# The causal mask of the first attention: added by VectorE on the way out of PSUM instead of accumulated by TensorE, with the reciprocal of the sums moved

## The chip, the cores and the metric

The kernel runs on one core of a Trainium2 chip. The metric is the device time of one execution in microseconds, the median of the timed runs; lower is better. A profiled execution records every instruction of every engine, and each of its durations and waits is taken from there.

## The reference, cut to what matters

Four blocks follow each other on an activation of 2048 tokens by 128 features: a windowed attention with global tokens, a memory layer, a second attention with rotary positions, and a mixture of experts. The change touches only the first attention. For the normalised input `x` (2048 x 128), 16 heads of 64 and windows of 128 tokens it is:

```
q, k, v = x @ wq, x @ wk, x @ wv                  # 16 heads of 64
gk, gv  = g_tok @ wk, g_tok @ wv                  # 32 global rows
att  = q_window @ k_window^T * SCALE              # 128 x 128 for each window and head
att  = where(upper triangle, neg, att)            # the causal mask
local_out  = softmax(att) @ v_window
global_out = softmax(q @ gk^T * SCALE) @ gv       # a softmax of its own, not masked
x = x + (local_out + global_out) @ wo
```

## The kernel before, in words

`attn0_block` works on 8 pairs of heads and 16 windows of 128 tokens: 128 steps, one for each pair and window. A round (`ROUND = 32`) is two pairs. Five engines each run their own list of instructions, written out by hand in the same order of steps (`step(r, i)`), and semaphores hold them together. There is no planner: the order in the code is the order on each engine, and an engine that waits holds up everything behind it in its list.

What step `i` does, engine by engine:

- **TensorE** (`pe`): the scores of window `i` for the two heads of the pair (L345: two products of 128 queries with 160 columns, 128 local keys and 32 global ones, each in its own PSUM bank, issued as four instructions since float32 takes two each). Then the mask (L349): four bf16 products of a split identity with a split mask matrix, which add -1e30 above the diagonal into the same banks. Then the transposes of the probabilities of window `i-2` (L363), the product of the probabilities of window `i-3` with the values (L375 and L377, called PV below), the output projection of window `i-4` (L388), and in 12 of 16 steps a piece of the q, k or v projection of the next pair (L326, L329, L322; `job`). The first of these 12 has the projection of the global rows in front (L315, L316). The last pair has no next one, so its 16 steps have no such piece.
- **VectorE** (`dve`): first the piece of k or v that the step before projected (L464, L472). Then it waits for the scores and takes the negated row maxima of the local part (L488, 256 elements in each partition, both heads) and of the global part (L489, 64 elements). In the one step per pair with global rows it saves them (`save_globals`, L456 and L458). Then the reciprocal of the sums of window `i-1` (L497), for which it waits for ScalarE's exponentials of that window; the copy of the transposed probabilities of window `i-2` (L503); and in every fourth step the addition to `x` (L510).
- **ScalarE** (`act`): a piece of q if there is one (L535). Then it waits for the maxima of window `i` and computes four exponentials with their sums: for each head the local one (L548, 128 elements, read from PSUM) and the global one (L550, 32 elements), each followed by the read-out of its sum. After them the copy of the output of window `i-3` out of its single PSUM bank (L558, `oT`).
- **GpSimd** (`pool`): multiplies the probabilities by the reciprocals (L580), both parts, and so releases the transposes.

The waits that matter here: the scores of step `i` overwrite the banks of step `i-2` and wait for its exponentials. PV of step `i` writes the one output bank and so waits until ScalarE has copied the output of PV of the step before, which stands in ScalarE's list behind the exponentials of the step before:

```
    pe.wait_ge(pt_saved, r * ROUND + w + 1)
    if w >= 1:
        pe.wait_ge(o_saved, r * ROUND + w)          # PV of window w, in step w + 3
```

and in ScalarE's list

```
    mm.then_inc(exp_ready, 1)                       # the four exponentials of window i
    w = i - 3
    act.wait_ge(o_ready, r * ROUND + w + 1)
    nc.scalar.activation(oT[:, w % 4, :], m.psum[:, O_B, 0:P], ACT.Copy).then_inc(o_saved, 1)
```

The first q piece of a pair waits until VectorE has saved the global rows (`g_saved`), as it uses the same PSUM bank. `setup_block` fills the constants on GpSimd while SyncE issues the first loads.

Of the kernel before, what the change touches and what calls it, by code (L numbers as in the profile page):

```python
# [7 lines left out]
BF16 = mybir.dt.bfloat16  # L8
# [3 lines left out]
ALU = mybir.AluOpType  # L12
# [138 lines left out]
def setup_block(nc, m, a):  # L151

    with ExitStack() as ctx:
# [25 lines left out]
        def _(pool):  # L179
            nc.gpsimd.memset(m.ident[:, :], 0.0).then_inc(zeroed, 1)  # L180
            nc.gpsimd.memset(m.identb[:, :], 0.0).then_inc(zeroed, 1)
            nc.gpsimd.memset(m.split_ident[:, :, :], 0.0).then_inc(zeroed, 1)
            nc.gpsimd.memset(m.split_mask[:, :, :], 0.0).then_inc(zeroed, 1)
# [3 lines left out]
            pool.wait_ge(zeroed, 7)  # L187
            for c in range(NC):
                nc.gpsimd.memset(m.wo_last[c * VCOLS:c * VCOLS + 1, D:D + 1], 1.0).then_inc(zeroed, 1)
            pool.wait_ge(zeroed, 11)  # L190
# [5 lines left out]
            for part in range(2):  # L196
                for g0 in (0, P // 2):
                    rows = slice(g0, g0 + P // 2)
                    pool.wait_ge(patterned, 2 + 2 * (2 * part + g0 // (P // 2)))
                    i, w = m.split_ident[rows, part, :], m.split_mask[rows, part, :]  # L200
                    nc.gpsimd.affine_select(out=i, in_=i, compare_op=ALU.not_equal, fill=1.0,
                                            base=part * P // 2, pattern=[[-1, P]], channel_multiplier=1).then_inc(patterned, 1)
                    nc.gpsimd.affine_select(out=w, in_=w, compare_op=ALU.is_ge, fill=MASKED,
                                            base=part * P // 2, pattern=[[-1, P]], channel_multiplier=1).then_inc(patterned, 1)


def attn0_block(nc, m, a, loads):
# [3 lines left out]
    with ExitStack() as ctx:  # L211
        def sb(name, shape, dt=F32):
            return ctx.enter_context(nc.sbuf_tensor(name, shape, dt))
# [11 lines left out]
        nmax = sb("nmax", [P, 4, 4])  # L225
        total = sb("total", [P, 4, 4])
# [23 lines left out]
        max_ready, exp_ready = sem("max_ready"), sem("exp_ready")  # L250
# [58 lines left out]
        def _(pe):  # L309
# [22 lines left out]
            def step(r, i, more=True):  # L332
                if i < ROUND or more:
# [10 lines left out]
                    for j in range(2):  # L344
                        nc.tensor.matmul(m.psum[:, bank + j, 0:WL], qs[half[j], b, s * P:(s + 1) * P], kx[half[j], b, s, :],  # L345
                                         start=True, stop=False)
                    for part in range(2):
                        for j in range(2):
                            mm = nc.tensor.matmul(m.psum[:, bank + j, 0:P], m.split_ident[half[j], part, :],  # L349
                                                  m.split_mask[half[j], part, :], start=False, stop=(part == 1))  # L350
# [123 lines left out]

# [1240 lines left out]
```

## Time and profile before

| what | value |
|---|---|
| runs shown, us | 1282.47, 1283.92, 1284.54 (median 1283.92) |
| the profiled execution, its own time | 1284.34 us |
| its span | 1282.6 us |
| TensorE busy in the span | 1224.7 us (95%) |
| first attention, from its first scores to its last step | 28.6 to 360 us |
| granted clock of TensorE from 28.6 to 33, from 33 to 36, from 50 to 340 us | 1.00, 0.54, 1.00 |
| TensorE busy from 28.6 to 33 us | 2.24 of 4.40 us |
| set-up: SyncE's last issue ends, GpSimd's last select ends | 5.95 us, 5.99 us |

The span runs from the first to the last recorded instruction, and the execution's own time is 1.74 us longer. Busy time is what an engine spent in instructions; a share near 100% says that an engine is full, not that it does nothing needless. In the timeline each row has a start, a duration and, in brackets, the idle time ahead of it with the instruction that ended it. The instructions of one line that follow each other are merged into one row with their count; the duration then runs from the first start to the last end. Consecutive instructions of VectorE and ScalarE overlap a little: the next one starts before the recorded end of the last.

### The profile page before, as it was taken

The page shows a single profiled execution, that of the slowest core. Times are in us where ns is not written, and L with a number is a line of the kernel's source. Part 1 is how long each engine was busy: PE and PEld are TensorE (multiplying, and loading weights), DVE is VectorE, ACT ScalarE, POOL GpSimd, SP SyncE. Part 2 cuts the span into 40 slices and gives each one's busy share as a digit, 9 for nine tenths or more (in the row PEclk, how much of TensorE's full clock was granted, in tenths as well). Part 3 has the DMA queues.
Part 4 walks back from the last instruction along what each step waited for, and adds up shares of the span by engine and source line. Part 5 has one row for each costly group of instructions (what it writes and reads, how often), then busy time and mean ns, then how long its engine had stood idle before and what let it go on. Part 6 is the DMA issues. An engine that isn't in the chain of part 4 may idle for free. (4 is left out here: it accounts for less than half of the span.)

```text
span 1282.6 us, 26536 instructions
## 1 busy us (share of the span) xinstructions
PE 1224.7 (95%) x10153; PEld 667.2 (52%) x10153; DVE 975.1 (76%) x1668; ACT 878.0 (68%) x2401; POOL 185.7 (14%) x366
## 2 busy tenths in 40 slices
PE   6999999999986879999999999999999999998999
PEld 5777777777864643433333333333333333334677
DVE  6666666666677869899999999999999999935300
ACT  3566566666746520488888888888888888885542
POOL 2333333333354130000000000010000000000100
PEclk9999999999997985699999999999999999999999
DMA  3100000000000030001110001100011000000100
GB/s 83 74 10 10 7 4 10 10 1 4 2 1 1 1 146 35 27 20 47 38 39 29 24 27 39 38 29 23 27 38 39 30 24 25 22 6 1 37 17 17
DMA packets 24891, 34.04 MB, mean 27 GB/s; under 512 B 6685, under 2 KB 18749, under 8 KB 22526
## 3 DMA queue, kind: packets, MB, share of 16 engines
q1 hardware_dynamic: 24766, 32.35, 7.6%
q8 instruction: 81, 1.33, 0.5%
q14 instruction: 44, 0.36, 0.1%
HBM read 24.86 MB, written 5.24 MB: 23 GB/s over the span
## 5 line engine op out<-in xcount | busy, mean ns | idle before, releaser
L1231 DVE TENSOR_REDUCE rowmax<-psum 128x1 f32<-128x1024 f32 x512 | 618.0, 1224 | 29.8 <-PE psum L1094 22.3
L1336 ACT ACTIVATE pb<-psum 128x512 f32<-128x512 f32 x1024 | 555.7, 596 | 78.9 <-PE psum L1136 58.3
L1094 PE MATMUL psum<-kf,qf 64*128 64x512 f32 x1024 | 393.0, 467 | 5.0 <-DVE rowmax L1231 3.9
L1136 PE MATMUL psum<-qf,kf 64*128 64x512 f32 x1024 | 377.1, 448 | 0.8 <-DMA qf<-nT 0.8
L1121 PE MATMUL psum<-pb,vx 128*32 128x256 f32 x4096 | 327.4, 392 | 3.6 <-issue 3.6
L1136 PEld LDWEIGHTS psum<-qf,kf 64*128 64x128 f32 x1024 | 153.7, 186 | 209.4 <-ACT pb L1336 190.8
L1121 PEld LDWEIGHTS psum<-pb,vx 128*32 128x32 f32 x4096 | 81.4, 108 | 188.5 <-ACT pb L1336 96.8
L1094 PEld LDWEIGHTS psum<-kf,qf 64*128 64x128 f32 x1024 | 161.3, 195 | 29.7 <-DVE rowmax L1231 24.4
L548 ACT ACTIVATE pr<-psum,nmax 128x128 f32<-128x128 f32 x256 | 93.8, 366 | 114.4 <-DVE nmax L489 114.3
L580 POOL TENSOR_TENSOR pr<-pr,rtotal 128x256 f32<-128x256 f32 (+1 forms) x256 | 110.5, 452 | 235.9 <-DVE rtotal L497 235.9
L488 DVE TENSOR_REDUCE nmax<-psum 128x2 f32<-128x256 f32 x128 | 53.8, 420 | 65.0 <-PE psum L349 65.0
L1370 POOL CAST nparts<-nfull 128x16 fp32r<-128x16 f32 x16 | 3.1, 196 | 623.7 <-DVE nfull L1240 623.7
L377 PE MATMUL psum<-pt,vz 128*128 128x128 f32 x512 | 78.5, 276 | 0.0
L550 ACT ACTIVATE pr<-psum,nmax 128x32 f32<-128x32 f32 x256 | 73.0, 285 | 0.0
L345 PE MATMUL psum<-kx,qs 64*128 64x160 f32 x512 | 69.8, 350 | 1.7 <-ACT pr L550 1.7
L363 PE MATMUL psum<-ident,pr 128*128 128x128 f32 x384 | 70.4, 292 | 0.7 <-POOL pr L580 0.7
L503 DVE COPY pt<-psum 128x384 f32<-128x384 f32 x128 | 67.9, 531 | 1.8 <-PE psum L363 1.6
L377 PEld LDWEIGHTS psum<-pt,vz 128*128 128x128 f32 x512 | 67.9, 193 | 0.0
L345 PEld LDWEIGHTS psum<-kx,qs 64*128 64x128 f32 x512 | 38.8, 185 | 52.9 <-ACT pr L550 39.2
L1523 ACT ACTIVATE hT<-psum,b 128x512 f32<-128x512 f32 x48 | 32.4, 688 | 40.6 <-PE psum L1538 40.5
L550 ACT ACTIVATION_READ_ACCUMULATOR pr<-psum,nmax 128x1 f32 x256 | 53.0, 207 | 0.0
L375 PE MATMUL psum<-pt,gv 128*128 128x128 f32 x256 | 51.4, 283 | 0.3 <-ACT oT L558 0.2
(220 smaller groups left out, 1370.7 us busy)
## 6 DMA issues: line engine op xcount, KB each, us to landing
qf<-q_parts SPq DMA_DIRECT2D x62, 128.0 KB
kf<-k_parts SPq DMA_DIRECT2D x62, 128.0 KB
k_parts<-parts SPq DMA_DIRECT2D x4, 512.0 KB, 3.3
q_parts<-parts SPq DMA_DIRECT2D x4, 512.0 KB, 3.9
x<-in_L_attn_x SPq DMA_DIRECT2D x2, 512.0 KB, 4.7
cos<-cos_table SPq DMA_DIRECT2D x1, 1024.0 KB
sin<-sin_table SPq DMA_DIRECT2D x1, 1024.0 KB
sumsT<-acc SPq DMA_DIRECT2D x60, 16.0 KB
```

The costliest lines, as they stand in the source:

```text
L345: nc.tensor.matmul(m.psum[:, bank + j, 0:WL], qs[half[j], b, s * P:(s + 1) * P], kx[half[j], b, s, :], start=True, stop=False)
L363: mm = nc.tensor.transpose(m.psum[:, T_B, j * P:(j + 1) * P], pr[:, w % 4, j * P:(j + 1) * P], m.ident[:, :])
L377: mm = nc.tensor.matmul(ob, vz[:, b, j, s, :], pt[:, w % 2, j * P:(j + 1) * P], start=False, stop=(j == 1))
L503: nc.vector.tensor_copy(pt[:, w % 2, :], m.psum[:, T_B, 0:TW]).then_inc(pt_saved, 1)
L548: nc.scalar.activation(pr[:, i % 4, j * P:(j + 1) * P], sc[:, 0:P], ACT.Exp, bias=nmax[:, i % 4, j:j + 1], accum_out=total[:, i % 4, j:j + 1])
L550: mm = nc.scalar.activation(pr[:, i % 4, 2 * P + j * G0:2 * P + (j + 1) * G0], sc[:, P:WL], ACT.Exp, bias=nmax[:, i % 4, 2 + j:3 + j], acc ...
L580: mm = nc.gpsimd.tensor_tensor(prw, prw, rb, ALU.mult)
L1094: mm = nc.tensor.matmul(m.psum[:, M_B + (u % 2) * 2 + n % 2, :], qf[ROWS, b, t * P:(t + 1) * P], kf[ROWS, b, c * BANK:(c + 1) * BANK], sta ...
L1121: mm = nc.tensor.matmul(m.psum[c * VCOLS:(c + 1) * VCOLS, A_B, cols], vx[:, h % VB, t, :], pb[:, (h * NT + t) % 3, c, cols], start=(t == 0 ...
L1136: nc.tensor.matmul(m.psum[:, bank, :], kf[SCORES, b, t * P:(t + 1) * P], qf[SCORES, b, c * BANK:(c + 1) * BANK], start=True, stop=True).th ...
L1231: nc.vector.tensor_reduce(rowmax[:, g % 2, u // 2, u % 2:u % 2 + 1], m.psum[:, M_B + (u % 2) * 2:M_B + (u % 2) * 2 + 2, :].rearrange("p b ...
L1336: nc.scalar.activation(pb[:, s % 3, c, :], m.psum[:, bank_of[(s, c)], :], ACT.Exp, scale=SCALE).then_inc(exp_ready, 1)
```

## The change

The mask is no longer multiplied in by TensorE. A float32 mask of 128 x 128 (0 and -1e30) is built once. In each step VectorE adds it to the local scores of both heads as it reads them from PSUM and writes the masked scores to a new SBUF tile, `masked` (four windows deep). Behind this addition stands the reciprocal for window `i-1`, which stood behind the maxima (and behind `save_globals`). Then come the maximum of the global part from PSUM and the maximum of the local part, now from `masked`, for which VectorE waits on a semaphore of its own addition. The order of the two maxima is swapped. ScalarE's local exponentials read `masked` in SBUF instead of PSUM; its global ones are as before. The rest of the block is as it was.

```diff
@@ setup_block, gpsimd
-            nc.gpsimd.memset(m.split_ident[:, :, :], 0.0).then_inc(zeroed, 1)
-            nc.gpsimd.memset(m.split_mask[:, :, :], 0.0).then_inc(zeroed, 1)
+            nc.gpsimd.memset(m.mask[:, :], 0.0).then_inc(zeroed, 1)
...
-            for part in range(2):
-                for g0 in (0, P // 2):
...
-                    nc.gpsimd.affine_select(out=i, in_=i, compare_op=ALU.not_equal, fill=1.0, ...
-                    nc.gpsimd.affine_select(out=w, in_=w, compare_op=ALU.is_ge, fill=MASKED, ...
+            pool.wait_ge(patterned, 2)
+            nc.gpsimd.affine_select(out=m.mask[:, :], in_=m.mask[:, :], compare_op=ALU.is_ge, fill=MASKED,
+                                    base=0, pattern=[[-1, P]], channel_multiplier=1).then_inc(patterned, 1)
@@ attn0_block, tensor, step
                     for j in range(2):
-                        nc.tensor.matmul(m.psum[:, bank + j, 0:WL], qs[half[j], b, s * P:(s + 1) * P], kx[half[j], b, s, :],
-                                         start=True, stop=False)
-                    for part in range(2):
-                        for j in range(2):
-                            mm = nc.tensor.matmul(m.psum[:, bank + j, 0:P], m.split_ident[half[j], part, :],
-                                                  m.split_mask[half[j], part, :], start=False, stop=(part == 1))
+                        mm = nc.tensor.matmul(m.psum[:, bank + j, 0:WL], qs[half[j], b, s * P:(s + 1) * P], kx[half[j], b, s, :],
+                                              start=True, stop=True)
                     mm.then_inc(scores_ready, 1)
@@ attn0_block, vector, step
+            def invert_sums(r, i, more):
+                w = i - 1
+                if 0 <= w < ROUND or (w >= ROUND and more):
+                    dve.wait_ge(exp_ready, r * ROUND + w + 1)
+                    nc.vector.reciprocal(rtotal[:, w % 4, :], total[:, w % 4, :]).then_inc(rtotal_ready, 1)
...
-                    nc.vector.tensor_reduce(nmax[:, i % 4, 0:2], smw[:, :, 0:P], AX_X, ALU.max, negate=True)
-                    nc.vector.tensor_reduce(nmax[:, i % 4, 2:4], smw[:, :, P:WL], AX_X, ALU.max,
+                    nc.vector.tensor_tensor(masked[:, i % 4, :, :], smw[:, :, 0:P],
+                                            m.mask[:, :].rearrange("p (o k) -> p o k", o=1).broadcast_to([P, 2, P]),
+                                            ALU.add).then_inc(masked_ready, 1)
+                invert_sums(r, i, more)
+                if i < ROUND or more:
+                    nc.vector.tensor_reduce(nmax[:, i % 4, 2:4], smw[:, :, P:WL], AX_X, ALU.max, negate=True)
+                    dve.wait_ge(masked_ready, r * ROUND + i + 1)
+                    nc.vector.tensor_reduce(nmax[:, i % 4, 0:2], masked[:, i % 4, :, :], AX_X, ALU.max,
                                             negate=True).then_inc(max_ready, 1)
                 if job(i, more) and job(i, more)[1:] == (0, "q"):
                     save_globals(r, job(i, more)[0], J_B)
-                w = i - 1
-                if 0 <= w < ROUND or (w >= ROUND and more):
-
-                    dve.wait_ge(exp_ready, r * ROUND + w + 1)
-                    nc.vector.reciprocal(rtotal[:, w % 4, :], total[:, w % 4, :]).then_inc(rtotal_ready, 1)
@@ attn0_block, scalar, step
-                        nc.scalar.activation(pr[:, i % 4, j * P:(j + 1) * P], sc[:, 0:P], ACT.Exp,
+                        nc.scalar.activation(pr[:, i % 4, j * P:(j + 1) * P], masked[:, i % 4, j, :], ACT.Exp,
                                              bias=nmax[:, i % 4, j:j + 1], accum_out=total[:, i % 4, j:j + 1])
```

## Rows read from the trace of the kernel before

**Rows 1.** Busy time by stretch; columns as in the first line.
```profile
core 0: us, PE busy (x) PEld busy (x) DVE busy (x) ACT busy (x) POOL busy (x), PEclk, DMA share, GB/s
50.00:340.00 290.00, 290.00 (x2429) 224.94 (x2428) 177.54 (x564) 181.34 (x1014) 94.62 (x220) 1.00 0.02 6
...
375.00:380.00 5.00, 4.16 (x17) 1.37 (x18) 4.16 (x18) 3.00 (x5) 4.08 (x3) 1.00 0.02 5
```

**Rows 2.** Timeline of a step without a projection: start, duration, engine, line.
```profile
202.03 0.30 PEld L375 LDWEIGHTS psum<-pt,gv 128*128 128x128 f32 x2
...
203.12 0.54 PE L345 MATMUL psum<-kx,qs 64*128 64x160 f32 x4
...
203.49 0.28 PE L349 MATMUL psum<-split_mask,split_ident 64*128 64x128 bf16 x4
...
203.70 0.55 PE L363 MATMUL psum<-ident,pr 128*128 128x128 f32 x3
203.81 0.42 DVE L488 TENSOR_REDUCE nmax<-psum 128x2 f32<-128x256 f32 x1 [1.03 <-PE psum L349]
...
204.15 0.21 DVE L489 TENSOR_REDUCE nmax<-psum 128x2 f32<-128x64 f32 x1
...
204.28 0.17 DVE L497 RECIPROCAL rtotal<-total 128x4 f32<-128x4 f32 x1
...
204.40 0.37 ACT L548 ACTIVATE pr<-psum,nmax 128x128 f32<-128x128 f32 x1 [0.61 <-DVE nmax L489]
...
205.07 0.54 PE L345 MATMUL psum<-kx,qs 64*128 64x160 f32 x4
...
205.53 0.21 ACT L550 ACTIVATION_READ_ACCUMULATOR pr<-psum,nmax 128x1 f32 x1
205.62 0.29 ACT L558 ACTIVATE oT<-psum 128x128 f32<-128x128 f32 x1
...
206.02 0.30 PEld L375 LDWEIGHTS psum<-pt,gv 128*128 128x128 f32 x2
```

**Rows 3.** Timeline: scores and local maxima behind a k piece, then a v piece.
```profile
213.47 0.54 PE L345 MATMUL psum<-kx,qs 64*128 64x160 f32 x4
...
214.19 0.41 DVE L488 TENSOR_REDUCE nmax<-psum 128x2 f32<-128x256 f32 x1
...
216.32 0.54 PE L345 MATMUL psum<-kx,qs 64*128 64x160 f32 x4
...
217.10 0.42 DVE L488 TENSOR_REDUCE nmax<-psum 128x2 f32<-128x256 f32 x1
```

**Rows 4.** Timeline of the step with global rows, and the next scores.
```profile
208.50 0.69 DVE L456 COPY kx<-psum 128x512 f32<-128x512 f32 x1
...
209.11 0.43 DVE L458 COPY gv<-psum 32x64 f32<-32x64 f32 x2
...
209.60 0.30 PEld L326 LDWEIGHTS psum<-xnT,w_cur 128*128 128x128 f32 x2
...
210.66 0.54 PE L345 MATMUL psum<-kx,qs 64*128 64x160 f32 x4
```

**Rows 5.** Timeline: scores of the second step of two neighbouring pairs, 16 steps apart.
```profile
201.00 0.54 PE L345 MATMUL psum<-kx,qs 64*128 64x160 f32 x4
...
243.72 0.54 PE L345 MATMUL psum<-kx,qs 64*128 64x160 f32 x4
```

**Rows 6.** Groups of the whole span by shape: busy us, mean ns | idle before.
```profile
L1503 DVE TENSOR_TENSOR x<-x,psum 128x256 f32<-128x256 f32 x2 | 0.8, 421 | 19.9 <-PE psum L1550 19.9
...
L1240 DVE TENSOR_REDUCE nfull<-rowmax 128x16 f32<-128x32 f32 x16 | 3.0, 186 | 0.6
...
L128 ACT ACTIVATE xnT<-psum 128x512 f32<-128x512 f32 x12 | 6.7, 599 | 6.9 <-PE psum L147 6.9
L909 ACT ACTIVATE parts<-rot 128x512 fp32r<-128x512 f32 x8 | 5.0, 630 | 20.0 <-DVE rot L902 20.0
```

**Rows 7.** Timeline of the filling: first exponentials, first q piece of pair 1.
```profile
29.92 0.37 ACT L548 ACTIVATE pr<-psum,nmax 128x128 f32<-128x128 f32 x1 [1.10 <-DVE nmax L489]
...
38.80 1.04 PE L326 MATMUL psum<-xnT,w_cur 128*128 128x512 f32 x2
```

More of the change, by code:

```diff
@@ L186, in _ @@
             nc.gpsimd.memset(m.uw2_cols[:, :], 0.0).then_inc(zeroed, 1)
-            pool.wait_ge(zeroed, 7)
+            pool.wait_ge(zeroed, 6)
             for c in range(NC):
                 nc.gpsimd.memset(m.wo_last[c * VCOLS:c * VCOLS + 1, D:D + 1], 1.0).then_inc(zeroed, 1)
-            pool.wait_ge(zeroed, 11)
+            pool.wait_ge(zeroed, 10)
             nc.gpsimd.affine_select(out=m.ident[:, :], in_=m.ident[:, :], compare_op=ALU.not_equal, fill=1.0,
@@ L194, in _ @@
                                     base=0, pattern=[[-1, P]], channel_multiplier=1).then_inc(patterned, 1)
-            for part in range(2):
-                for g0 in (0, P // 2):
[L198 to L204, printed above, removed]
+            pool.wait_ge(patterned, 2)
+            nc.gpsimd.affine_select(out=m.mask[:, :], in_=m.mask[:, :], compare_op=ALU.is_ge, fill=MASKED,
+                                    base=0, pattern=[[-1, P]], channel_multiplier=1).then_inc(patterned, 1)
 def attn0_block(nc, m, a, loads):
@@ L225, in attn0_block @@
         nmax = sb("nmax", [P, 4, 4])
+        masked = sb("masked", [P, 4, 2, P])
         total = sb("total", [P, 4, 4])
@@ L249, in attn0_block @@
         scores_ready = sem("scores_ready")
-        max_ready, exp_ready = sem("max_ready"), sem("exp_ready")
+        masked_ready, max_ready, exp_ready = sem("masked_ready"), sem("max_ready"), sem("exp_ready")
         rtotal_ready, probs_ready = sem("rtotal_ready"), sem("probs_ready")
@@ L1597, in build @@
         m.ones = sb("ones", [P, P])
-        m.split_ident = sb("split_ident", [P, 2, P], BF16)
-        m.split_mask = sb("split_mask", [P, 2, P], BF16)
+        m.mask = sb("mask", [P, P])
         m.ws1 = sb("ws1", [P, UH])
```

## The prediction

> **What bounds the kernel now.** I read the busy time by stretch first. From 50 to 340 us, inside the first attention, TensorE is busy for all of 290 us at a granted clock of 1.00, VectorE for 178 and ScalarE for 181 [rows 1]. The reader is to see a full TensorE, and that taking work off it looks like pure gain. So the second view is the timeline of one step, because a full engine and a chain of waits of the same length look alike in a busy share.
>
> In the step without a projection piece the two are level. Unhindered, TensorE goes from scores to scores in 1.95 us (203.12 to 205.07). The other thing that can set the pace is a chain through three engines [rows 2]: the weight load of PV at 202.03; TensorE gets from there to the next scores in 1.09; from scores to the first maximum 0.69; from there to the start of the exponentials 0.59 (204.40); from there to the end of the output copy that stands behind them 1.51 (205.91); and 0.11 later the weight load of the PV of two steps on, 206.02. That is 3.99 us for two steps, 2.00 each. I call it the **output loop**. Each single PV waits for it: TensorE's own 1.95 is 0.05 below.
>
> In a step with a piece TensorE needs 2.81 (k, 210.66 to 213.47) or 2.85 (v, to 216.32) [rows 3, 4]. I take q as k, since it is the same product turned round. A piece thus adds 0.86 or 0.90 to 1.95. The loop gets the piece once for two steps, 3.99 + 0.9 = 4.9 against 5.6, so there TensorE alone sets the pace. Sixteen steps take 42.72 us (201.00 to 243.72) [rows 5].
>
> **What the change takes away.** The four mask products: the transposes start 0.21 us behind the first of them [rows 2]. TensorE's own floors become 1.74 (no piece), 2.60 (k, q) and 2.64 (v). If nothing else counted, 128 steps would save 128 x 0.21 = 27 us.
>
> **What it adds, on VectorE between scores and exponentials.** The scores of 203.12 are recorded to end 0.54 later, the masks 0.65 (203.77), and VectorE starts 0.04 behind that. Without masks I put its start at 0.58 behind the scores instead of 0.69.
> - The addition, 256 elements from PSUM and SBUF: the nearest row is an addition of this very shape with 421 ns [rows 6]. Bounds: 0.37 and 0.47, a spread of one eighth either way for the other destination and the repeated mask.
> - The overlap of neighbours on VectorE is 0.08 (0.42 recorded, the next starts 0.34 later; 0.21 recorded, next 0.13 later) [rows 2]. So the addition occupies 0.34, the reciprocal 0.17 - 0.08 = 0.09, the global maximum 0.13.
> - The local maximum from SBUF: not in the trace. Two PSUM rows (64 elements 0.21, 256 elements 0.42 [rows 2]) give 1.09 ns an element and 0.18 for 32 elements; the SBUF row of 32 elements says 186 ns [rows 6]. So memory makes no difference in the rows and I take 0.42. Bounds: 0.31 (if SBUF went at two elements in the time of one: 0.19 + 224 x 0.55 ns) and 0.47.
> - The two new waits. That for the addition's own result is over when the global maximum has been issued (0.56 behind the addition's start, its end at 0.42), so I give it nothing; up to 0.1 if a wait drains the engine. That of the moved reciprocal for the exponentials of the step before is treated below.
>
> From scores to exponentials: 0.58 + 0.34 + 0.09 + 0.13 + 0.42 + 0.04 = 1.60, against 1.28 now: 0.32 longer.
>
> **ScalarE.** Two of the four exponentials now read SBUF. An activation of 512 elements takes 630 ns from SBUF and 599 from PSUM [rows 6], so 0.03 more each, 0.06 a step (bounds 0 and 0.10). Exponentials 1.40 instead of 1.34 (204.40 to 205.74), to the end of the output copy 1.57 instead of 1.51.
>
> Two statements of the Trainium skill bear on this. "VectorE: DVE Perf Modes", section on the TRN2 errata, gives VectorE a fixed 58 cycles for an SBUF source and 120 for a PSUM one; by that the local maximum would be about 0.065 us cheaper than I take it, an estimate from that page. The rows disagree with it: 0.18 against 186 ns at 32 elements. The same table gives ScalarE 52 cycles more for SBUF, 0.043 us an activation, where the row has 0.031; by the page the sum would be 0.02 a step dearer there. Together the page would shorten the loop by about 0.04 us for two steps, a gain of some 3 us over all.
>
> **The output loop afterwards.** No piece: 1.09 + 1.60 + 1.57 + 0.11 = 4.37 for two steps. With a q piece in the first of them + 0.86 = 5.23. With k: VectorE first copies the piece and starts 0.72 behind the scores [rows 3] whether masks are there or not, 0.14 later than 0.58, so 5.37. With v it starts at 0.78, so 4.37 + 0.90 + 0.20 = 5.47. Halves: 2.19, 2.62, 2.69, 2.74. **All lie above TensorE's floors.** The engine that was full is released and the loop takes its place at once: without a piece the step becomes longer than now (2.19 for 2.00), with a piece shorter, but only by some 0.14 of the 0.21.
>
> There is a second loop, new: exponentials of step i-1, reciprocal, global maximum, local maximum, exponentials of step i, since the reciprocal now stands ahead of the maxima: 0.04 + 0.09 + 0.13 + 0.42 + 0.04 + 1.40 = 2.12 for one step. I call it the **serial loop**. It is under 2.19, but by little. In piece steps it is under 2.6 and plays no part.
>
> **One pair, 16 steps.** I set each PV at the later of (PV before + TensorE's floor) and (PV two steps before + loop), from the first step behind the global rows. Pieces come k v q: 0, 2.60 (floor), 5.37 (loop), 8.07 (loop), 10.67 (floor), 13.44, 16.14: 8.07 us for three steps. So PV 9 steps on is 24.21, then 26.81, 29.58; 32.28 (26.81 + 5.47, behind the last v); 34.02 (floor); 36.65 (loop). Scores 1.09 behind it, 37.74. The step with global rows: local maximum over at 1.56, copies of the global rows (0.61 and 0.43 [rows 4]) from 1.48 to 2.52, weight load of q 0.06 later, next scores 1.06 behind (209.60 to 210.66): 3.64. Next scores at 41.38; the starting ones stood 0.74 ahead of the first PV (0.37 + 0.37 to the transposes and past them), so 42.12 us for a pair against 42.72: **-0.60**.
>
> **The sum.** Six such pairs -3.6. The last run of 11 piece steps: 26.81 + 1.09 + 0.90 + 0.74 = 29.54 against 7 x 2.81 + 4 x 2.85 = 31.07: -1.5. The last 15 steps have no piece: 15 x (4.37 - 3.99)/2 = +2.85, with the passage into them +3.0. The filling: first exponentials 0.42 later, 30.34, and then one each 2.12 by the serial loop, the fifth at 38.82. Global rows saved from 38.70 to 39.74, q piece at 39.88 against 38.80 [rows 7]: +1.1. The draining +0.3 (0.32 once). The set-up: seven selects fewer on GpSimd, nothing gained, as SyncE's last issue ends level with them (5.95 and 5.99); its cover is those loads, and without them it would be 2 us. The moved reciprocal gives GpSimd its start some 0.25 us earlier; the transposes have slack there, so nothing. Sum: -3.6 - 1.5 + 3.0 + 1.1 + 0.3 = **-0.7 us**. Against the profiled execution's 1284.34 that is 1283.6; the median shown is 0.4 below that execution, so I say **1283.2**.
>
> How firm is it: every 0.1 us on the loop is 0.05 a step, 6.4 us over 128 steps upward; downward TensorE's floors catch part of it.
>
> **The rivals.**
> - **Shorter link.** The local maximum at its lower bound, 0.31: piece steps settle near 2.63 (-0.06 x 84 = -5), the 44 others at 2.13 (-2.4), the filling -0.4. With -0.7 that is -8.5: 1275.5. For it: nothing on VectorE's rows. The fixed costs that the Trainium skill gives in "VectorE: DVE Perf Modes", section on the TRN2 errata, point that way at half the size.
> - **TensorE stays the bound.** The whole 0.21 in the 84 piece steps (-17.6) and 0.05 in the 44 others (-2), if the exponentials' delay were hidden: 1265. Against it: the loop reproduces 3.99 exactly as it is now.
> - **The serial loop decides (slower).** The reciprocal waits for the exponentials in front of the maxima. It decides once it passes 2.19, that is with 0.07 more on its links: a wait of VectorE that drains the engine (0.1 each for two waits) makes it 2.32, and the output loop 0.2 longer. Then +0.13 x 44 and +0.1 x 84: +14, 1297; with half of that 1290. For it: only 0.07 us of slack, and waits that are met today cost nothing only where their result is long there.
> - **The clock (slower).** TensorE would be idle for 0.44 of 2.19 us in steps without a piece. Now it is full at 1.00 [rows 1]; from 28.6 to 33 us it was busy 2.24 of 4.40 us, and from 33 to 36 the granted clock was 0.54. If the clock falls to 1.2 GHz, its 1.74 becomes 3.5, 1.3 us a step lost; twice in each of 7 pairs is +18 less what the steps absorb, say 1296. Against it: 4.16 of 5 us busy kept 1.00 [rows 1], and 1.74 of 2.19 is almost that share.
> - **A cheaper addition or nothing gained by removing masks**: within the forecast's own range.
>
> **How the numbers follow.** Forecast 0.52 (its own range 1279.5 to 1287), shorter link 0.20, TensorE bound 0.06, serial loop 0.13, clock 0.09. About 0.2% or 2.6 us is what a measurement can tell from no change, 1281.3 to 1286.5. Faster: a quarter of the forecast's case, nearly all of the next two, 0.37. Slower: an eighth of the first, nearly all of the last two, 0.26. Same 0.37. Range 1274 to 1292.
>
> **What would show it.** Right: TensorE no longer 100% busy between 50 and 340 us; its weight load for PV with idle time that the output copy L558 ended; steps without a piece near 2.19 and with one near 2.69; exponentials starting 1.60 behind the scores; the addition near 0.42 and the local maximum near 0.42. Wrong: piece steps at 2.6 (a shorter link, or no loop), steps without a piece at 2.3 or with the reciprocal's wait ended by the exponentials (serial loop), a granted clock under 1.00 between 50 and 340. The forecast falls if the maxima are ready less than 0.2 us later than now.

## The result

Slightly slower, and by enough runs to tell it from no change. The kernel after has a median of 1287.16 us (20 runs, 1285.28 to 1288.67), the kernel before, run beside it, 1284.36 (20 runs, 1282.35 to 1288.87). The ratio is 1.0019 with an interval of 1.0012 to 1.0027, which is +2.4 us (+1.5 to +3.5); the forecast was -0.7. The profiled execution of the kernel after took 1286.48 us, its span 1284.7, against 1284.34 and 1282.6 before.

The window of 290 us inside the first attention, kernel after (columns as in [rows 1]):

```profile
50.00:340.00 290.00, 283.92 (x1998) 210.60 (x1996) 212.66 (x678) 186.89 (x1017) 95.26 (x220) 1.00 0.02 6
```

Against [rows 1] TensorE has 6 us of idle time where it had none, VectorE 35 us more work, ScalarE 5.5 us more, and the granted clock is 1.00 as before. The groups of the changed instructions, kernel after (busy us, mean ns | idle before, and what ended most of it):

```profile
L546 ACT ACTIVATE pr<-masked,nmax 128x128 f32<-128x128 f32 x256 | 101.2, 395 | 113.7 <-DVE nmax L492 113.7
L485 DVE TENSOR_TENSOR masked<-psum,mask 128x256 f32<-128x256 f32 x128 | 53.7, 420 | 47.2 <-PE psum L339 47.2
L548 ACT ACTIVATE pr<-psum,nmax 128x32 f32<-128x32 f32 x256 | 68.9, 269 | 0.0
L492 DVE TENSOR_REDUCE nmax<-masked 128x2 f32<-128x256 f32 x128 | 52.4, 409 | 0.0
```

A step without a piece, kernel after, to be laid beside [rows 2]; scores are L339 now, transposes L353, PV L365, output copy L556:

```profile
204.91 0.54 PE L339 MATMUL psum<-kx,qs 64*128 64x160 f32 x4
...
205.38 0.55 PE L353 MATMUL psum<-ident,pr 128*128 128x128 f32 x3
...
205.50 0.42 DVE L485 TENSOR_TENSOR masked<-psum,mask 128x256 f32<-128x256 f32 x1 [0.68 <-PE psum L339]
...
205.84 0.17 DVE L470 RECIPROCAL rtotal<-total 128x4 f32<-128x4 f32 x1
205.93 0.19 DVE L490 TENSOR_REDUCE nmax<-psum 128x2 f32<-128x64 f32 x1
206.04 0.41 DVE L492 TENSOR_REDUCE nmax<-masked 128x2 f32<-128x256 f32 x1
...
206.11 0.46 PE L365 MATMUL psum<-pt,gv 128*128 128x128 f32 x2 [0.18 <-ACT oT L556]
...
206.48 0.40 ACT L546 ACTIVATE pr<-masked,nmax 128x128 f32<-128x128 f32 x1 [0.52 <-DVE nmax L492]
...
207.17 0.54 PE L339 MATMUL psum<-kx,qs 64*128 64x160 f32 x4
207.28 0.69 DVE L508 TENSOR_TENSOR x<-x,psum 128x512 f32<-128x512 f32 x1 [0.36 <-PE psum L378]
...
207.64 0.41 PE L309 MATMUL psum<-gtok,w_cur 128*128 128x32 f32 x2
...
207.88 0.42 DVE L485 TENSOR_TENSOR masked<-psum,mask 128x256 f32<-128x256 f32 x1
```

The reader is to see three things. From scores to exponentials it now takes 1.57 us (204.91 to 206.48) where it took 1.28. PV now has idle time that the output copy ended (206.11). And the transposes start 0.47 behind the scores (204.91 to 205.38) where they started 0.58 behind: **only 0.11 us has gone, though 0.21 lay between the first mask product and the transposes.**

Behind a k piece, kernel after, beside [rows 3]:

```profile
213.58 0.54 PE L339 MATMUL psum<-kx,qs 64*128 64x160 f32 x4
...
213.76 0.27 ACT L556 ACTIVATE oT<-psum 128x128 f32<-128x128 f32 x1
214.05 0.31 PEld L353 LDWEIGHTS psum<-ident,pr 128*128 128x128 f32 x3 [0.17 <-issue]
...
214.33 0.30 PEld L365 LDWEIGHTS psum<-pt,gv 128*128 128x128 f32 x2
...
216.32 0.41 PE L339 MATMUL psum<-kx,qs 64*128 64x160 f32 x2
```

The output copy is over at 214.03, and PV's weight load follows the transposes at 214.33 with no idle time in brackets. In a piece step nothing but TensorE's own list sets the pace.

Where the time went, all read from the starts of the scores. "First scores" is step 0 of the first attention.

| stretch | before | after | difference | forecast |
|---|---|---|---|---|
| filling, first scores to the sixth | 11.20 | 12.55 | +1.35 | +1.1 |
| one pair, 16 steps (six of them) | 42.72 | 42.46 | -0.26 | -0.60 |
| of it the 11 piece steps | 31.10 | 29.88 | -1.22 | -1.56 |
| of it the step with global rows | 3.55 | 3.71 | +0.16 | +0.09 |
| of it the 4 steps without a piece | 8.07 | 8.87 | +0.80 | +0.87 |
| last run of 11 piece steps | | | -1.2 | -1.5 |
| last 15 steps | 30.05 | 33.07 | +3.02 | +3.0 |
| draining, last scores to last addition to x | 7.46 | 7.81 | +0.35 | +0.3 |

With six pairs (-1.6) the differences sum to +2.0, and the two spans differ by 2.1. The forecast's column sums to -0.7, so 2.7 is to be explained, and 0.34 x 7 = 2.4 of it lies in the piece steps. The row of the filling is the least firm: it stands on one profile of each kernel, and the last step of the filling alone took from 3.5 to 6.3 us in the profiles of the runs below (3.91 before, 4.02 after). The rows of a pair repeat from pair to pair within 0.01 us.

### The profile page after: what moved, and what is told of

It reads as the page before. It is cut to its first block and busy times, and to the rows that moved or that the text cites. A ratio compares the mean times of both kernels' runs of the same rounds, so it can differ in the third digit from the quotient of the medians.

```text
span 1284.7 us, 25625 instructions
## 1 busy us (share of the span) xinstructions
PE 1217.0 (95%) x9641; PEld 647.5 (50%) x9641; DVE 1015.2 (79%) x1796; ACT 884.3 (69%) x2401; POOL 184.0 (14%) x358
## 5 line engine op out<-in xcount | busy, mean ns | idle before, releaser
L546 ACT ACTIVATE pr<-masked,nmax 128x128 f32<-128x128 f32 x256 | 101.2, 395 | 113.7 <-DVE nmax L492 113.7
L485 DVE TENSOR_TENSOR masked<-psum,mask 128x256 f32<-128x256 f32 x128 | 53.7, 420 | 47.2 <-PE psum L339 47.2
L339 PE MATMUL psum<-kx,qs 64*128 64x160 f32 x512 | 70.3, 352 | 2.4 <-ACT pr L548 2.3
L353 PE MATMUL psum<-ident,pr 128*128 128x128 f32 x384 | 70.6, 293 | 0.6 <-POOL pr L578 0.6
L548 ACT ACTIVATE pr<-psum,nmax 128x32 f32<-128x32 f32 x256 | 68.9, 269 | 0.0
L339 PEld LDWEIGHTS psum<-kx,qs 64*128 64x128 f32 x512 | 39.1, 187 | 53.9 <-issue 37.4
L365 PE MATMUL psum<-pt,gv 128*128 128x128 f32 x256 | 52.4, 286 | 7.9 <-ACT oT L556 7.7
L492 DVE TENSOR_REDUCE nmax<-masked 128x2 f32<-128x256 f32 x128 | 52.4, 409 | 0.0
```

What stands on the lines that cost most here:

```text
L339: mm = nc.tensor.matmul(m.psum[:, bank + j, 0:WL], qs[half[j], b, s * P:(s + 1) * P], kx[half[j], b, s, :], start=True, stop=True)
L353: mm = nc.tensor.transpose(m.psum[:, T_B, j * P:(j + 1) * P], pr[:, w % 4, j * P:(j + 1) * P], m.ident[:, :])
L546: nc.scalar.activation(pr[:, i % 4, j * P:(j + 1) * P], masked[:, i % 4, j, :], ACT.Exp, bias=nmax[:, i % 4, j:j + 1], accum_out=total[:, ...
L548: mm = nc.scalar.activation(pr[:, i % 4, 2 * P + j * G0:2 * P + (j + 1) * G0], sc[:, P:WL], ACT.Exp, bias=nmax[:, i % 4, 2 + j:3 + j], acc ...
```

## The experiments

Interval figures are ratios to the kernel before in runs on the same chip, and a difference in us is such a ratio of 1284.4. The median of before was 1285.98 beside no mask, half, twice and mask on both, 1285.11 beside the four runs that move the reciprocal or the output copy, and 1286.25 beside the small product and the transposes by part. Steps are read from the starts of the scores in each run's profile.

### What do the mask products cost TensorE?

**No mask at all** (the kernel before; the causal mask is left out of the computation).

```
-                        nc.tensor.matmul(... qs ..., kx ..., start=True, stop=False)
-                    for part in range(2):
-                        for j in range(2):
-                            mm = nc.tensor.matmul(... split_ident ..., split_mask ..., start=False, stop=(part == 1))
+                        mm = nc.tensor.matmul(... qs ..., kx ..., start=True, stop=True)
```

> The kernel before with the four mask products left out and nothing put in their place (no mask is applied: the exponentials and maxima see all 128 keys). It is the TensorE half of the change alone. Theory A (two heads side by side): the four products run as two pairs, each pair in the time of one, 0.055 us, and the 0.09 us between the last of them and the transposes is there without them too. Then the transposes start 0.47 us behind the scores instead of 0.58, a step with a k or q piece takes 2.70 us, with a v piece 2.74, one without a piece 1.94 (output loop 3.99 - 0.11 for two). 84 x 0.11 + 44 x 0.09 = 13 us less than before: 1271. Theory B (my prediction's step: 0.21 us go): transposes at 0.37, piece steps 2.60 and 2.64, 84 x 0.21 + 4 = 22 us less: 1262.

1276.05 us, ratio 0.9924 [0.9899, 0.9948]: -9.8 us. From this run, two steps of the timeline:

```profile
251.55 0.54 PE L345 MATMUL psum<-kx,qs 64*128 64x160 f32 x4
252.02 0.55 PE L359 MATMUL psum<-ident,pr 128*128 128x128 f32 x3
...
254.29 0.41 PE L345 MATMUL psum<-kx,qs 64*128 64x160 f32 x2
```

The transposes stand 0.47 behind the scores, not 0.37, and that step (v) takes 2.74 us, not 2.64; k and q steps take 2.70. Theory A's sizes for the piece steps are met exactly, and theory B's 22 is out of the question. Its size for the steps without a piece is not met: they take 2.00 us on average in the pairs and 1.98 in the last run of steps, where 1.94 was expected (2.02 and 2.00 in the kernel before). The output loop takes 3.90 for two steps, but 4.02 to 4.08 for the two around an addition to x. With 84 x 0.11 + 44 x 0.02 = 10 us the 9.8 is accounted for.

**Half the mask products** (only the first part of the split mask; the other part is left out of the computation).

```
-                    for part in range(2):
-                        for j in range(2):
-                            mm = nc.tensor.matmul(... split_ident[half[j], part, :], split_mask[half[j], part, :], stop=(part == 1))
+                    for j in range(2):
+                        mm = nc.tensor.matmul(... split_ident[half[j], 0, :], split_mask[half[j], 0, :], stop=True)
```

> The kernel before with two of the four mask products (part 0 of the split only, so half of the mask is left out). Theory A: one pair of 0.055 us goes: transposes 0.53 us behind the scores, k step 2.76, v step 2.80; 84 x 0.055 + 44 x 0.04 = 6 us less than before, 1278. Theory B (0.053 us for each product, one after the other, and no fixed gap): two products give 0.105, transposes at 0.475, k step 2.71: 11 us less, 1273.

**Mask products twice** (the mask is added twice).

```
-                    for part in range(2):
+                    for part in range(4):
...
-  split_ident[half[j], part, :], split_mask[half[j], part, :], stop=(part == 1)
+  split_ident[half[j], part % 2, :], split_mask[half[j], part % 2, :], stop=(part == 3)
```

> The kernel before with the mask products issued twice (eight instead of four; the values above the diagonal become -2e30 instead of -1e30, the rest is unchanged). Theory A: two more pairs, +0.11 a step: transposes 0.69 us behind the scores, k step 2.92, step without a piece 2.05: 84 x 0.11 + 44 x 0.04 = 11 us more than before, 1295. Theory B: +0.21 a step, transposes at 0.79, k step 3.02, 84 x 0.21 + 44 x 0.1 = 22 us more, 1306.

1280.68 us, 0.9957 [0.9940, 0.9974], which is -5.5 where theory A had -6, and 1296.35 us, 1.0082 [1.0059, 1.0105], which is +10.5 where it had +11. First the run with half, then the run with twice as many:

```profile
251.28 0.54 PE L345 MATMUL psum<-kx,qs 64*128 64x160 f32 x4
251.66 0.22 PE L348 MATMUL psum<-split_mask,split_ident 64*128 64x128 bf16 x2
251.81 0.55 PE L362 MATMUL psum<-ident,pr 128*128 128x128 f32 x3
```

```profile
253.86 0.54 PE L345 MATMUL psum<-kx,qs 64*128 64x160 f32 x4
254.24 0.39 PE L349 MATMUL psum<-split_mask,split_ident 64*128 64x128 bf16 x8
254.56 0.55 PE L363 MATMUL psum<-ident,pr 128*128 128x128 f32 x3
```

From scores to transposes: 0.47 with none, 0.53 with two, 0.58 with four [rows 2, 203.12 to 203.70], 0.70 with eight. That is 0.47 plus 0.028 for each product, a straight line whose constant is 0.10 above the 0.37 at which the first mask product starts. So four products occupy 0.11 us: the two heads' products lie on different halves of the rows and run side by side, 0.055 for each two. The Trainium skill, "TensorE: Matmul & The Clock Gate", section "Part 3: Packing small matmuls", says that products on distinct groups of rows run concurrently; the line above agrees. The remaining 0.10 is there with and without them.

**A small product in the gap** (the kernel after; one needless product of 32 columns between scores and transposes, into unused PSUM columns).

```
                         pe.wait_ge(pt_saved, r * ROUND + w)
+                    nc.tensor.matmul(m.psum[:, T_B, TW:TW + 32], m.ident[:, :], pr[:, w % 4, 0:32], start=True, stop=True)
                     for j in range(3):
```

> The changed kernel with one small extra product (identity, 128 rows, 32 columns, two instructions as float32) issued between the scores and the transposes, into 32 unused columns of the transposes' bank. It asks what the 0.09 us belong to that TensorE loses between the scores and the transposes (0.47 us from scores to transposes, of which the products themselves fill 0.37). Theory S (the gap belongs to the change from the scores' tiles of 64 rows to tiles of 128 rows): the extra product starts 0.47 behind the scores, that is the gap stands in front of it, and the transposes follow it without a gap of 0.09. Theory T (the gap belongs to the transposes): the extra product starts at 0.38 and the gap stands behind it. The time itself: two instructions of 32 columns, 0.05 to 0.1 us a step, 84 steps: 4 to 8 us more than the changed kernel, 1291 to 1295.

One run of 1306.04 us, where 1291 to 1295 was expected; a single run says little by its total, its timeline does:

```profile
204.40 0.54 PE L339 MATMUL psum<-kx,qs 64*128 64x160 f32 x4
204.87 0.41 PE L352 MATMUL psum<-pr,ident 128*128 128x32 f32 x2
205.12 0.52 PE L354 MATMUL psum<-ident,pr 128*128 128x128 f32 x3
...
207.32 0.41 PE L339 MATMUL psum<-kx,qs 64*128 64x160 f32 x2
```

The gap now stands in front of the small product (0.47 behind the scores), and the transposes follow it without one (0.25 later, which its two instructions fill at some 0.11 to 0.12 each). So the gap is not one of the transposes: it stands in front of the first product on all 128 rows behind the 64-row scores. In the step with global rows that is the projection of the global rows, and it too starts 0.47 behind (207.17 to 207.64 above).

Two other readings have to be looked at. That float32 makes the gap: no. In the filling of the kernel after the scores of two steps follow each other, all of them float32 on 64 rows, and the second four add 0.27 us to the 0.54 of the first (granted clock 1.00 from 28.4 to 29.3 us):

```profile
28.47 0.81 PE L339 MATMUL psum<-kx,qs 64*128 64x160 f32 x8
```

That a semaphore wait makes it: the small product stands behind the same two waits as the transposes, so this run can't tell. PV has two waits in front of it as well, and its weight load follows the transposes without a gap (214.33 above), so a satisfied wait costs nothing there. But in the first attention every 128-row product right behind 64-row ones has a wait in front, in all runs. That the change of rows alone makes the gap is therefore likely, and not shown.

The size was missed: piece steps grew to 2.92 and 2.96, by 0.22 where 0.05 to 0.1 was expected, and 84 x 0.22 = 18.5 us above the kernel after is near this run's time. The steps without a piece did not grow in sum (2.09, 2.26, 2.37 in the last run, as in the kernel after): 0.22 us more work on TensorE is free there, so TensorE does not set their pace.

The waits view of the kernel after over the whole span (engine line waited for: us in total, times, longest us) has the weight load of the transposes idle 117 times for 0.17 us each, counted from the recorded end of the scores' last weight load. Its second line belongs to the serial loop and is used below:

```profile
PEld psum L353 <- issue: 20.1, 117, 0.2
...
DVE rtotal L470 <- ACT pr L548: 4.9, 10, 1.1
```

### What do the additions cost?

**Mask on both** (the kernel after with the mask products put back, so the mask is added twice).

```
+                    for part in range(2):
+                        for j in range(2):
+                            mm = nc.tensor.matmul(... split_ident ..., split_mask ..., start=False, stop=(part == 1))
```

> The changed kernel with the four mask products back on TensorE as well (the mask is added twice, -2e30 above the diagonal). It is the VectorE and ScalarE half of the change alone. Output-loop theory: a step without a piece becomes (4.35 + 0.10)/2 = 2.23 us, as VectorE starts 0.69 instead of 0.59 behind the scores; piece steps stay bound by TensorE at 2.81 and 2.85 as before, since their loop (5.2 to 5.5 for two) fits under 5.62. Filling +1.35, global step +0.2 in each of 7 pairs, 44 x 0.2 = 9: about 12 us more than before, 1296. The rival that VectorE's longer list sets the pace of the piece steps too: they rise above 2.81, by 0.1 each another 8 us, 1304.

1299.55 us, 1.0106 [1.0084, 1.0128]: +13.6 us, where 12 was expected. Piece steps 2.81 and 2.85 again, steps without a piece in the last run 2.09 and 2.37 in turn, 2.23 on average. Removal alone gives -9.8 and the rest of the change alone costs +13.6; their sum, +3.8, is within the intervals of the +2.4 measured for both.

**Reciprocal last** (the kernel after, the reciprocal back behind the maxima and the saving of the global rows).

```
-                invert_sums(r, i, more)
                 if i < ROUND or more:
...
                     save_globals(r, job(i, more)[0], J_B)
+                invert_sums(r, i, more)
```

> The changed kernel with the reciprocal back behind the maxima and behind the saving of the global rows. It undoes the second half of the change. Output-loop theory: VectorE's part is 0.09 us shorter, so steps without a piece take (4.35 - 0.09)/2 = 2.13 instead of 2.2, and during the filling the exponentials no longer stand one behind the other 2.10 us apart (exponentials, reciprocal, maxima, exponentials), which takes about 1 us off; piece steps stay at 2.71: 1287.2 - 3 - 1 = 1283. Rival (the early reciprocal is worth something because GpSimd starts 0.4 us earlier and the transposes wait for it): the transposes would now wait for GpSimd, and the steps without a piece stay at 2.2 or grow: 1287 to 1290.

1285.86 us, 1.0001 [0.9991, 1.0012]. The filling falls to 11.44 us, a pair to 42.27, steps without a piece to 2.19 on average in the pairs and 2.16 in the last run of steps (2.22 and 2.20 in the kernel after), where 2.13 was forecast; 1283 us was expected. The rest went to a new wait: GpSimd gets the sums later, and some transposes wait for it, here in the last run of steps:

```profile
334.81 0.31 PEld L353 LDWEIGHTS psum<-ident,pr 128*128 128x128 f32 x3 [0.52 <-POOL pr L578]
```

**Output copy between the heads** (the kernel after; ScalarE copies the output behind the first head's two exponentials, not behind all four).

```
                     for j in range(2):
+                        if j == 1:
+                            copy_output(r, i, more)     # wait for o_ready, copy to oT
                         sc = m.psum[:, S_B + i % 2 * 2 + j, :]
...
-                w = i - 3
-                if 0 <= w < ROUND or (w >= ROUND and more):
-                    act.wait_ge(o_ready, r * ROUND + w + 1)
-                    nc.scalar.activation(oT[:, w % 4, :], m.psum[:, O_B, 0:P], ACT.Copy).then_inc(o_saved, 1)
```

> The changed kernel with ScalarE's copy of the output moved from behind the four exponentials to between the two heads, nothing else. It takes the output loop away (the copy ends 0.7 us earlier) and lengthens the exponentials by the copy, 0.18 us. If the output loop alone sets the steps without a piece, they fall from 2.2 to TensorE's 1.85: 44 x 0.35 = 15 us less than the changed kernel, 1272. If the serial loop of the moved reciprocal is next, as I now expect, it is 0.04 + 0.09 + 0.11 + 0.41 + 0.03 + 1.41 + 0.18 = 2.27 us a step and decides: 44 x 0.07 = 3 us more, 1290. Piece steps 2.71 in both.

1291.43 us, 1.0046 [1.0030, 1.0062]: slower than the kernel after. The output loop is cut, and the serial loop takes over with the copy now inside it. In the last run of steps:

```profile
341.38 0.18 DVE L470 RECIPROCAL rtotal<-total 128x4 f32<-128x4 f32 x1 [0.72 <-ACT pr L556]
...
342.03 0.40 ACT L554 ACTIVATE pr<-masked,nmax 128x128 f32<-128x128 f32 x1 [0.68 <-DVE nmax L492]
...
343.63 0.18 DVE L470 RECIPROCAL rtotal<-total 128x4 f32<-128x4 f32 x1 [0.72 <-ACT pr L556]
```

There every reciprocal waits for ScalarE and every exponential for VectorE, once round in 2.25 us; 2.27 was forecast. In a pair the four steps without a piece come to 8.39 us, less than the 8.87 of the kernel after, but the step with global rows takes 4.41 instead of 3.71, as its q piece waits for VectorE to save the global rows: 42.68 a pair for 42.46. These differences, with 0.1 in the last 15 steps and 0.8 in the draining, make 2.2 of the 3.5 us between the two kernels. In the two profiles the rest is in the filling (14.54 against 12.54 us), where single profiles scatter by as much.

**Both moves** (copy between the heads and reciprocal last: the two diffs above together).

> The changed kernel with both: the output copy between the heads and the reciprocal behind the maxima. Neither the output loop nor the serial loop is left. Next in line for a step without a piece is GpSimd's way: scores, addition, maxima, reciprocal at 1.37 us behind the scores, GpSimd from 1.62 to 2.48, transposes 0.1 later, next but one scores 1.39 behind these: 3.97 for two steps, 1.98 each. TensorE's floor is 1.85. Piece steps 2.71. 44 x (2.2 - 1.98) = 10 us less than the changed kernel, 1 from the filling, 1 from the global steps: 1275, which would beat the kernel before by 9. If some other wait replaces the loops (theory: VectorE's list is what counts), it stays at 2.1 or more: 1283.

1277.24 us, 0.9931 [0.9915, 0.9948]. Neither loop is left: steps without a piece average 2.01 in the pairs and 1.99 in the last run (forecast 1.98), piece steps 2.70 and 2.74, a pair 41.55. So the two loops cover each other. With each ratio turned into us against the kernel before (+2.4 for the kernel after), the copy move alone costs 3.5 us (+5.9), the reciprocal's move alone gives 2.3 (+0.1), and both together give 11 (-8.9). The first two have intervals of some 2 us either way; the 11 is clear of them.

**The copy move in the kernel before** (the same diff of ScalarE's list on the kernel before).

> The kernel before with the output copy between the two heads, nothing else. It says what the output loop cost before the change. Theory: steps without a piece fall from 2.00 (2.04 in pairs) to TensorE's 1.95, piece steps stay at 2.81: 44 x 0.06 = 3 us less than before, 1281.5. Rival (the exponentials' longer time of 0.18 us comes on top elsewhere): no change or slower, 1284 to 1286.

1283.30 us, 0.9984 [0.9971, 0.9997]: -2.1 us, where 1281.5 was forecast, with steps without a piece at 1.95 and 1.96. TensorE's floor stood just beneath the loop, as the prediction had it. Without the change the copy's place is worth 2 us, and with the change and the reciprocal last 9 (from +0.1 to -8.9). This is also the fair comparison of the two ways of masking: with the output copy out of the way in both, the kernel with the mask on VectorE (-8.9) is ahead of the one with the mask on TensorE (-2.1) by 7 us.

**Transposes by part** (both moves, and GpSimd signals the local part by itself, so that the two local transposes need not wait for the global part).

```
-                    pe.wait_ge(probs_ready, r * ROUND + w + 1)
+                    pe.wait_ge(probs_ready, 2 * (r * ROUND + w) + 1)
...
                     for j in range(3):
+                        if j == 2:
+                            pe.wait_ge(probs_ready, 2 * (r * ROUND + w) + 2)
...
-                        mm = nc.gpsimd.tensor_tensor(prw, prw, rb, ALU.mult)
-                    mm.then_inc(probs_ready, 1)
+                        nc.gpsimd.tensor_tensor(prw, prw, rb, ALU.mult).then_inc(probs_ready, 1)
```

> The version with the output copy between the heads and the reciprocal last, and in addition GpSimd signals the local part of the probabilities on its own, so that the two local transposes start before the global part is multiplied (0.25 us earlier). Theory (GpSimd's way sets the steps without a piece there, 3.95 us for two as measured): the way is 0.25 shorter, but the third transpose then waits for the global part, 0.22 behind the first: 0.2 us less for two steps, 1.88 each instead of 1.97, near TensorE's 1.85: 44 x 0.09 = 4 us less than that version, 1273. Rival (the wait is for the copy of the transposes or for the exponentials, not for GpSimd): no change, 1277.

1274.50 us, 0.9909 [0.9886, 0.9931], 1273 was expected: the best version, ahead of both kernels. Against the run with both moves the intervals overlap, and the gain shows in the steps. The wait that it takes away, first in the run with both moves, then in this one:

```profile
203.21 0.54 PE L339 MATMUL psum<-kx,qs 64*128 64x160 f32 x4
...
203.91 0.31 PEld L353 LDWEIGHTS psum<-ident,pr 128*128 128x128 f32 x3 [0.41 <-POOL pr L583]
...
205.29 0.54 PE L339 MATMUL psum<-kx,qs 64*128 64x160 f32 x4
```

```profile
332.02 0.54 PE L339 MATMUL psum<-kx,qs 64*128 64x160 f32 x4
...
332.49 0.35 PEld L355 LDWEIGHTS psum<-ident,pr 128*128 128x128 f32 x3 [0.17 <-POOL pr L585]
...
333.86 0.41 PE L339 MATMUL psum<-kx,qs 64*128 64x160 f32 x2
```

The transposes are back at 0.47 behind the scores instead of 0.70, and the 0.17 in brackets is the one that every transposes' weight load has there. Steps without a piece take 1.84 to 1.87, every fourth one 1.99 to 2.05, and a pair 41.13.

## Why the prediction was wrong, step by step

**What the change takes away: here it failed.** The prediction read 0.21 us from the first mask product to the transposes [rows 2] and called all of it the price of the mask products. It was the price of the products, 0.11, and of a gap, 0.10, that stands in front of whatever first uses all 128 rows behind the 64-row products, with masks or without. Zero, two, four and eight products show the line, the small product shows where the gap sits; what makes it is not shown. A distance between two starts contains everything between them, also what will be there for the next neighbour.

**TensorE's floors** were put at 1.74, 2.60 and 2.64 and are 1.85, 2.70 and 2.74. From this follows the second failure, the statement that all halves of the output loop lie above TensorE's floors. The loop with a v piece comes to 5.47 in two steps (5.45 with the 4.35 measured below), TensorE's own to 2.70 + 2.74 = 5.44, and with k or q the loop is shorter; so in piece steps TensorE still sets the pace, as no idle time in front of PV's weight load shows. The two answers were near each other by luck: the loop was to make 2.69 of a piece step, TensorE makes 2.72. That 0.03 in each of 77 steps is 2.4 of the 2.7 us by which the sum was off. If TensorE's true floors decide every piece step, 11 of them take 7 x 2.70 + 4 x 2.74 = 29.86 us; 29.88 were measured. A pair then gives -0.26, and the whole sum is -1.6 - 1.2 + 3.0 + 1.1 + 0.3 = +1.6 us, just inside the measured interval.

**The output loop** was right, place and size: forecast 4.37 us for two steps without a piece. In the kernel before it was misread in one point that does not touch the sum: not each PV waited for it, but every second. The PV of 203.98 follows its transposes by 0.28, as TensorE goes unhindered; that of 206.02 follows by 0.37:

```profile
203.98 0.30 PEld L375 LDWEIGHTS psum<-pt,gv 128*128 128x128 f32 x2
```

So the steps were 1.95 and 2.04 in turn, which is 3.99 for two. From the last run of steps of the kernel after:

```profile
355.19 0.26 ACT L556 ACTIVATE oT<-psum 128x128 f32<-128x128 f32 x1
...
355.59 0.46 PE L365 MATMUL psum<-pt,gv 128*128 128x128 f32 x2 [0.29 <-ACT oT L556]
...
359.94 0.46 PE L365 MATMUL psum<-pt,gv 128*128 128x128 f32 x2 [0.17 <-ACT oT L556]
```

4.35 us, of two steps of 2.09 and 2.26. The last 15 steps came out at +3.02 for +3.0 and the four in each pair at +0.80 for +0.87. Every fourth step was not seen: there the addition to x stands in VectorE's way and the mask addition starts 0.71 behind the scores instead of 0.59 (207.17 to 207.88 above), which makes one step 2.37 and the two around it 4.46.

**What the addition costs.** Scores to exponentials 1.57 for 1.60; scores to addition 0.59 for 0.58; addition 420 ns for 0.42; local maximum 409 ns for 0.42; exponentials 1.41 (204.39 to 205.80) for 1.40. The local maximum is 11 ns shorter from SBUF (409, against 420 from PSUM in the kernel before), where the Trainium skill, "VectorE: DVE Perf Modes", section on the TRN2 errata, gives 62 cycles of difference, by estimate from that page 0.065 us: the measurement decides. ScalarE's activation from SBUF is 29 ns dearer (395 against 366), near the row that was used (31) and below the 43 estimated from that page. Neither difference is SBUF's alone: in the same two profiles the global maximum, unchanged in shape and still from PSUM, went from 216 to 194 ns, and the global exponentials, also unchanged, from 285 to 269. The satisfied wait for the addition's own result costs nothing visible: the local maximum starts 0.11 behind the global one.

**The serial loop** was put at 2.12. It shows in the filling, where the output loop has not closed:

```profile
32.24 0.40 ACT L546 ACTIVATE pr<-masked,nmax 128x128 f32<-128x128 f32 x1 [0.68 <-DVE nmax L492]
...
33.69 0.18 DVE L470 RECIPROCAL rtotal<-total 128x4 f32<-128x4 f32 x1 [0.70 <-ACT pr L548]
...
34.34 0.40 ACT L546 ACTIVATE pr<-masked,nmax 128x128 f32<-128x128 f32 x1 [0.68 <-DVE nmax L492]
...
36.43 0.40 ACT L546 ACTIVATE pr<-masked,nmax 128x128 f32<-128x128 f32 x1 [0.68 <-DVE nmax L492]
...
40.04 1.05 PE L320 MATMUL psum<-xnT,w_cur 128*128 128x512 f32 x2
```

2.10 and 2.09 a step. The filling is +1.24 at the q piece (40.04 against 38.80 in [rows 7]) for +1.1. In the middle of the kernel this loop decides only now and then (the ten waits of reciprocals in the waits view above), as it is 0.08 under half of 4.35. The output copy between the heads gave it 0.15 more, and it did decide.

**The rivals.** Shorter link: no, the maximum took 409 ns, not 310. TensorE stays the bound at -19.6: right for piece steps in kind, wrong in size, since it gives 0.11 and not 0.21 a step, and wrong for the others. Serial loop as the bound for all: no, forecast as unlikely, made true only by moving the copy. Clock: no, 1.00 from 50 to 340 us and in the last run of steps. The slower side came neither from the serial loop nor from the clock but from the forecast's own case, a gain of 10 us and a loss of 14, where 0.1 us misread in one term turned the sign.

## What to carry to other kernels

When work is taken off a full engine, price it by varying its count (none, half, twice) or by how far its own instructions stand apart, not by the distance to the next instruction: a gap between two shapes stays when what lies in it goes. Where two loops through the same engines are level, try moving both links at once: one alone gained some 2 us, the other lost 3.5, both gained 11.

## What the runs showed of the hardware

- Between the last 64-row product and the first 128-row weight load TensorE had a gap of some 0.1 us (0.47 from scores to transposes with nothing between, where a 64-row product starts at 0.37). Up to eight 64-row bf16 products did not fill it but pushed it back (0.70 with eight). The next 128-row weight loads of the same step showed none.
- Two bf16 products of 128 columns on the two halves of the rows take 0.055 us together at a granted clock of 1.00. A float32 product of 32 columns with 128-row weights takes two instructions of some 0.11 to 0.12 us each (204.87 to 205.12), as much as the two of 128 columns of PV's first product (214.33 to 214.55 in the kernel after, from weight load to weight load). Its fewer columns saved nothing.
- The same code gets its clock back at different times in the filling. From 36 to 40 us the granted clock was 0.50 in the profiled run with both moves, 0.70 in the kernel after and 0.87 in the run with the transposes by part; the step with global rows that falls there lasts 3.5 to 4.0 us in six of the twelve profiled kernels and 5.9 to 6.3 in the other six. Single spans scatter by 2 us and more from it, and the run with the transposes by part also had 0.87 from 500 to 520 us, where the kernel after had 0.50; its span, 1268.1, is therefore not the measure of it, its median, 1274.50, is. The first of these windows is the run with both moves, the second that with the transposes by part:

```profile
36.00:40.00 4.00, 4.00 (x18) 3.05 (x18) 2.13 (x8) 2.06 (x13) 0.61 (x2) 0.50 0.98 412
```

```profile
36.00:40.00 4.00, 4.00 (x23) 2.64 (x22) 2.55 (x8) 2.59 (x14) 0.62 (x2) 0.87 0.95 393
```
